# A three-stage decoder kernel: selected rows by indexed DMA, a new order of the steps, scores on four row strips, and one table for exp and ln

## The chip, the cores and the metric

The kernel runs on one core of a Trainium2 chip. The metric is the device time of one execution in microseconds; the median of the runs is given. The core has five engines, each with its own instruction queue: TensorE (PE in the profile, PEld its weight loads), VectorE (DVE), ScalarE (ACT), GpSimd (POOL) and SyncE (SP), which only issues DMAs here.

## The reference

Sixteen independent sequences (batch rows) of 256 tokens by 256 features pass through three stages, all in float32.

```python
x = x + attn(layernorm(x), w_attn, w_proj)          # stage a: causal linear attention, 16 heads of 16
x = x + xattn(layernorm(x), ctx, ctx, W_diff, ...)  # stage b: divergence attention over tanh probabilities, exact-gelu MLP 256-1024-256
x = x + ffn(layernorm(x), w_router, W_qkv, ...)     # stage c: below

def ffn(x, ...):                                    # CAP = 128 of the 256 tokens of a row
    scores = x @ w_router
    _, idx = top_k(scores, CAP)                     # ranks the tokens, ties by the smaller index
    x_sel = take_along_axis(x, idx)
    h = rmsnorm(x_sel, g1); q, k, v = h @ W_qkv.T   # 16 heads of 16, causal softmax attention over the 128
    x_attn = softmax(mask(q @ k.T / 4)) @ v @ W_out.T
    h2 = rmsnorm(x_sel + x_attn, g2)
    x_ff = silu(h2 @ W1.T) * (h2 @ W2.T) @ W3.T     # 682 wide
    return x.at[idx].set(x_sel + x_attn + x_ff)     # the other tokens keep x
```

## The kernel before

A batch row has its 256 tokens as two blocks (TT) of 128 partitions. The work is cut into some 170 named steps, `a_...`, `b_...` and `c_...` by stage. One text, `ORDER`, lists all of them; every engine runs through this list and executes the steps that it has a function for, so the list fixes the order in each engine's queue, while the times follow from semaphores. The list is one round. In round i stage a works on row i, stage b on row i-1, stage c on row i-2, and each `+` behind a name moves the step one row further back. The rounds that fill and drain the pipeline are written out; the others are a loop (`rounds`). An engine executes its queue strictly in order, so a step that waits holds back all behind it.

Large products with weights (`a_q`, `a_k`, `a_val`, `a_proj`, `b_up_*`, `b_down_*`, `c_gu_*`, `c_ff_*`) are split in a high and a low part and made of three passes. The others are plain float32; each such matmul stands in the trace as two records. PSUM has eight banks: a0, a1, a2 for stage a, b0, b1 for b, c0, c1, c2 for c.

Stage c, to which most of the change belongs, does the top-k and the gather by matrices. `c_rscore` (L938) makes the router scores as a column, `c_sbc` (L1298) spreads them over the partitions, `c_before` (L950) compares all pairs with a mask for ties, and `c_rank` (L1308, L1311) adds up the comparisons on TensorE to the rank of each token, as a row and as a column. `c_sel` and `c_selu` (L958, L965, L967) build three selection matrices, one scaled by the rms. `c_ht` (L1319) multiplies the normalised rows by the scaled one, which gives the selected rows transposed. `c_qk`, `c_v` and `c_score_0/1` (L1351 the mask, L1356 the products, 32 rows of the array each) follow; a score step fills two banks for 8 of the 16 heads, `c_max` takes row maxima, `c_exp` (L652) makes exponentials with their sum, one instruction a head, and `c_etp`, `c_etput` transpose them for `c_att`. `c_xo` (L1393, L1398) puts the selected rows (by the unscaled matrix) and the output projection in one bank. After the gated feed-forward, `c_scat` (L1469) multiplies the result, in two parts, by the third matrix, and `c_done` (L1032) adds it to `c_ob` (L975), the rows that were not selected. SyncE stores the result of the row. `x2`, the input of stage c, is started by GpSimd in `b_kept` (L402).

Stage a's scores `a_score_0/1` (L1166) use four row strips and four banks at a time. `keep_clock` (L1475) issues matmuls whose result nobody reads, 14 at the start and others at the places in `WARM_AT`, all in the first and the last rounds.

ScalarE needs a table load (ACT_TABLE_LOAD) where it goes to a function that the table in force does not hold. In a round of the kernel before, these stand at `a_qout` (exp, L532), `b_log` (ln, L589), `b_sexp` (exp, L602) and `b_gelu_0` (gelu, L615); the tanh of `b_tanhk`, `b_tanhq` (L571) and `c_tanh` (L691) has none.

## Time and profile before

| | |
|---|---|
| median of 3 runs | 951.96 us (951.67 to 952.5) |
| span of the profiled execution | 947.8 us |
| busy: PE, PEld, DVE, ACT, POOL | 883.4, 750.3, 727.6, 595.2, 218.6 us |
| mean granted TensorE clock | 0.995 of full speed |
| DMA | 25.05 MB, 26 GB/s over the span |

The span is that of the profiled execution, from its first to its last instruction; the median is of other executions and includes what lies around the span, 4.2 us here. Busy time is the union of an engine's instructions; the time that one instruction takes is longer than its distance to the next where they overlap. "Idle before" is time in which the engine waited, and the name behind the arrow is what released it.

### The profile page before, as it was taken

How to read it: one execution, taken by the hardware profiler on the slowest of the kernel's cores; microseconds unless marked ns; L12 is line 12 of the kernel's file. 1: busy time of each engine (PE TensorE's matmuls, PEld its weight loads, DVE VectorE, ACT ScalarE, POOL GpSimd, SP SyncE). 2: the span in 40 equal slices, each digit the busy share in tenths (PEclk: the TensorE clock that was granted, in tenths of full speed). 3: DMA queues.
4: the chain of work that ended last, by engine and by line, in shares of the span. 5: the costliest groups of instructions: out<-in, count | busy, mean ns of one | idle time of the engine just before them, and what ended most of it. 6: DMA issues, size and time to landing. Idle time of an engine off the chain costs nothing.

```text
span 947.8 us, 21833 instructions
## 1 busy us (share of the span) xinstructions
PE 883.4 (93%) x7652; PEld 750.3 (79%) x7652; DVE 727.6 (77%) x1670; ACT 595.2 (63%) x1582; POOL 218.6 (23%) x379
## 2 busy tenths in 40 slices
PE   7888999999999999999999999999999999998987
PEld 4657797978879797887979788787979788786855
DVE  4878878787887878888787879788787878866342
ACT  4365757667574767657575766757576675745533
POOL 0215122121313122221312222231321222121100
PEclk9999999999999999999999999999999999999999
DMA  7220100101010100101010010101000010000000
GB/s 261 68 82 2 35 1 13 35 12 33 11 33 0 37 7 11 33 11 33 0 44 0 11 33 11 33 11 33 0 17 28 11 33 22 12 2 11 2 13 12
DMA packets 20465, 25.05 MB, mean 26 GB/s; under 512 B 1488, under 2 KB 18000, under 8 KB 20432
## 3 DMA queue, kind: packets, MB, share of 16 engines
q1 hardware_dynamic: 18992, 20.33, 6.6%
q10 hardware_dynamic: 1440, 4.28, 1.4%
q8 instruction: 20, 0.33, 0.1%
q14 instruction: 13, 0.11, 0.0%
HBM read 20.41 MB, written 4.19 MB: 26 GB/s over the span
## 4 chain that ended last, share of the span: by engine, by line
PE 64%; DVE 20%; ACT 7%; issue 7%; DMA 1%; POOL 0%; DVEq 0%; SPq 0%; ACTq 0%; POOLq 0%
PE bank L1064 21%; PE bank L1370 4%; PE bank L1166 4%; PE bank L1356 4%; PE bank L1331 3%; PE bank L1245 3%; PE bank L1253 3%; PE bank L1424 2%; DVE before L950 2%; ACT L615 2%; PE bank L1319 2%; PE bank L1184 2%; PE bank L1457 2%; PE bank L1080 2%; DVE prob L850 2%
## 5 line engine op out<-in xcount | busy, mean ns | idle before, releaser
L652 ACT ACTIVATE w_raw_or_stage_c<-bank,c_nmax 128x128 f32<-128x128 f32 x256 | 90.6, 375 | 12.3 <-DVE c_nmax L981 12.3
L615 ACT ACTIVATE prob<-bank,b_folded 128x256 f32<-128x256 f32 x128 | 53.7, 471 | 46.0 <-PE bank L1064 45.8
L981 DVE TENSOR_REDUCE c_nmax<-bank 128x4 f32<-128x512 f32 x64 | 43.5, 683 | 48.1 <-PE bank L1356 48.1
L809 DVE TENSOR_TENSOR a_s<-bank,const 128x512 f32<-128x512 f32 x112 | 71.8, 677 | 9.0 <-PE bank L1166 6.4
L729 DVE TENSOR_TENSOR b_s_lo<-prob,b_s_hi 128x512 fp32r<-128x512 f32 x64 | 54.2, 848 | 27.3 <-ACT b_s_hi L503 27.3
L426 POOL TENSOR_TENSOR a_tr_lo<-a_norm,a_tr_hi 128x512 fp32r<-128x512 f32 x16 | 21.0, 1310 | 216.9 <-ACT a_tr_hi L503 216.9
L402 POOL TENSOR_TENSOR x<-x,vectors_by_row 128x512 f32<-128x512 f32 x16 | 20.7, 1292 | 161.7 <-DVE w_raw_or_stage_c L975 161.7
L652 ACT ACTIVATION_READ_ACCUMULATOR w_raw_or_stage_c<-bank,c_nmax 128x1 f32 x256 | 55.1, 215 | 0.0
L799 DVE RECIPROCAL a_e<-a_e 128x512 f32<-128x512 f32 x16 | 53.4, 3340 | 0.0
L1064 PE MATMUL bank<-b_s_hi,w_mlp_hi 128*128 128x256 f32 x256 | 44.8, 298 | 4.8 <-ACT prob L615 4.6
L1475 PE MATMUL bank<-ones_bf 128*128 128x512 bf16 x164 | 46.7, 410 | 1.0 <-POOL ones_bf L400 1.0
L691 ACT ACTIVATE w_raw_or_stage_c<-bank,c_rms_half 128x384 f32<-128x384 f32 (+1 forms) x32 | 17.2, 537 | 47.7 <-PE bank L1072 43.7
L503 ACT ACTIVATE b_s_hi<-prob 128x512 fp32r<-128x512 f32 x64 | 40.4, 632 | 9.9 <-PE bank L1064 9.3
L503 ACT ACTIVATE w_raw_or_stage_c<-bank 128x512 f32<-128x512 f32 x32 | 19.1, 598 | 43.7 <-PE bank L1370 43.7
L1370 PE MATMUL bank<-const,w_raw_or_stage_c 128*128 128x128 f32 x256 | 41.0, 283 | 2.0 <-ACT c_et L503 0.7
L1064 PEld LDWEIGHTS bank<-b_s_hi,w_mlp_hi 128*128 128x128 f32 x256 | 34.5, 189 | 10.2 <-ACT prob L615 8.8
L402 POOL TENSOR_TENSOR q_bias<-b_f,vectors_by_row 128x512 f32<-128x512 f32 x16 | 20.9, 1305 | 86.6 <-DVE b_f L875 86.6
L1370 PEld LDWEIGHTS bank<-const,w_raw_or_stage_c 128*128 128x128 f32 x256 | 27.5, 141 | 16.8 <-issue 12.3
L1064 PE MATMUL bank<-w_mlp_hi,b_s_lo 128*128 128x256 f32 x256 | 40.2, 279 | 0.0
L1064 PE MATMUL bank<-b_s_lo,w_mlp_hi 128*128 128x256 f32 x256 | 40.1, 279 | 0.0
L1064 PE MATMUL bank<-w_mlp_hi,b_s_hi 128*128 128x256 f32 x256 | 40.1, 278 | 0.0
L1064 PE MATMUL bank<-w_mlp_lo,b_s_hi 128*128 128x256 f32 x256 | 40.1, 278 | 0.0
(257 smaller groups left out, 2818.4 us busy)
## 6 DMA issues: line engine op xcount, KB each, us to landing
x_in<-in_x SPq DMA_DIRECT2D x16, 256.0 KB, 2.7
qc<-in_ctx SPq DMA_DIRECT2D x16, 256.0 KB, 3.2
b_f<-in_ctx_t SPq DMA_DIRECT2D x16, 256.0 KB, 3.4
out<-w_raw_or_stage_c SPq DMA_DIRECT2D x16, 256.0 KB, 2.1
w_raw_or_stage_c<-in_w ACTq DMA_DIRECT2D x4, 512.0 KB, 5.4
w_raw_or_stage_c<-in_w_gu ACTq DMA_DIRECT2D x4, 341.0 KB, 3.0
w_raw_or_stage_c<-in_w_a SPq DMA_DIRECT2D x2, 384.0 KB, 4.5
w_raw_or_stage_c<-in_w ACTq DMA_DIRECT2D x2, 384.0 KB, 4.4
```

What stands on the lines that cost most here:

```text
L402: add_bc = lambda out_, in_, vec: nc.gpsimd.tensor_tensor(out_, in_, vec.unsqueeze(1).broadcast_to([P, TT, D]), ALU.add)
L503: act_in(out_, in_, ACT.Copy, scale=scale).then_inc(done.sem, 1)
L615: act_in(prob[:, 2 * (j % 2) + n, :], b0[:, n * T:(n + 1) * T], ACT.Gelu, bias=b1p[:, f:f + 1]).then_inc(b_gelu.sem, 1)
L652: act_in(c_e[g % 2][:, j * R:(j + 1) * R], (c1, c2)[g % 2][:, j * R:(j + 1) * R], ACT.Exp, bias=c_nmax[:, n:n + 1], accum_out=c_den[:, hea ...
L729: tt(out_, full, high.bitcast(F32), ALU.subtract).then_inc(done.sem, 1)
L799: nc.vector.reciprocal(a_e1[:, :], a_e1[:, :]).then_inc(a_dinv.sem, 1)
L809: tt(heads(A_MASKED[t][n][:, :]), heads(A_SCORES[n][:, :]), tri.unsqueeze(1).broadcast_to([P, 4, P]), ALU.mult).then_inc(a_scput.sem, 1)
L981: nc.vector.tensor_reduce(c_nmax[:, 4 * g:4 * g + 4], heads((c1, c2)[g % 2][:, :]), axis=AX.X, op=ALU.max, negate=True).then_inc(c_max.sem, 1)
L1064: last = mm(out_, lhs(o, p, k), rhs(o, q, k), start=begin and a == 0 and o == 0 and k == 0, stop=end and a == len(passes) - 1 and k == n - ...
L1166: last = mm(A_SCORES[n][:, 2 * c * P:2 * (c + 1) * P], kT[r:r + 32, c, t * P:(t + 1) * P], qM[r:r + 32, c, t, :, :].rearrange("p m q -> p ...
L1370: last = nc.tensor.transpose(c0[:, j * R:(j + 1) * R], c_e[g % 2][:, j * R:(j + 1) * R], ident)
L1475: mm(heads((c2 if i < B else a0)[:, :]), ones_bf[:, :], ones_bf[:, :].unsqueeze(1).broadcast_to([P, 4, P]), start=True, stop=True)
```

## The change

The ranks are now made on VectorE alone: `c_rank` compares and adds up in one instruction for each token block. `c_sel` makes one selection matrix in bf16, and `c_idx` multiplies it by the token numbers, which gives the token number of each slot. SyncE stores normalised rows, residual rows and the rms, side by side, to a buffer in DRAM (`store_rows`, 256 rows of 513 numbers); GpSimd fetches the 128 selected ones by an indirect DMA (`c_pick`). `c_hsc` scales them and `c_ht` transposes them. The base of the output, `c_ob`, is now made on GpSimd for all tokens and stored as soon as it is there, and the 128 results are written over it by a second indirect DMA (`c_put`). `c_hx` on GpSimd adds the residual that goes with them; `c_h2put` moves from ScalarE to VectorE. The scores are made in one step on four row strips into the banks c0, c1, c2 and a2; this makes `a_k` and the score step wait for steps of other rows. `a_qout` asks for the table that holds exp and ln. `WARM_AT` is empty. `ORDER` is new, and its greatest shift is one more, so there is one more round. SyncE's queue has a new order too.

```diff
 ORDER = """
-a_y+ c_w2 c_att+ b_up_1+ b_down_0+ b_up_2+ c_dput+ b_gelu_1+ a_yhi+ b_ghi_1+ a_mean c_o+ b_glo_1+ c_w3 c_w0
-b_gelu_2+ a_done+ c_xo+ c_h2put+ c_h2lo+ b_mean b_ghi_2+ c_h2hi+ b_gelu_3+ a_proj+ b_glo_2+ a_normed b_ghi_3+
-c_w4 c_h2tp+ b_glo_3+ c_gate_0+ b_normed b_kept+ b_o+ b_omean+ c_gate_1+ b_fb2+ a_kept+ b_frstd+ b_up_3+
-b_down_1+ c_gu_0+ a_ylo+ c_h2rms+ c_gtlo_0+ a_rstd b_onormed+ b_down_2+ b_down_3+ c_gu_1+ b_tanhk b_rstd
-c_tanh_0+ b_qb c_tanh_1+ c_gu_2+ c_gthi_0+ c_gtp_0+ c_gtp_1+ c_ff_0+ a_tp b_done+ c_gthi_1+ a_thi c_gtlo_1+
-c_mean a_tlo c_y+ b_tanhq c_ff_1+ b_v b_pnorm c_ylo+ c_yhi+ b_vput c_normed a_q c_scat+ a_k a_qout c_sbc
-c_done+ b_orstd+ c_rscore a_kout b_diff c_before a_val c_rank b_log b_dtp a_ktp a_phi_q a_phi_k c_sel a_vput
-c_hput b_vq c_ht b_rtp b_ratio c_qk c_selu a_csum b_sid c_score_0 b_dput a_kput a_kq c_ob c_max_0 b_rput
-a_mask a_sput c_qkput b_sexp a_state c_exp_0 c_max_1 b_fput c_w5 a_dput b_fmean a_scput_0 a_scput_1 a_den b_fd
-c_v c_exp_1 c_vput c_w6 c_etput_0 a_scput_2 a_score_0 c_etp_0 c_score_1 a_scput_3 c_w7 c_w1 c_etp_1 c_max_2
-c_etput_1 a_score_1 b_htp b_fnormed a_att_0 c_etp_2 c_exp_2 c_w8 a_scput_4 b_hhi c_max_3 b_hlo c_rstd c_rms1
-a_scput_5 a_scput_6 c_dinv b_up_0 a_scput_7 c_exp_3 c_etput_2 c_etp_3 a_dinv c_dtp c_dbc c_etput_3 b_glo_0
-b_gelu_0 b_ghi_0 c_w9 a_att_1
+c_w2 a_kput+ c_ff_0++ c_ff_1++ c_gtlo_1++ c_rstd+ c_ht+ a_score_0+ b_fput+ b_fmean+ b_htp+ a_sput+ c_hsc+
+b_sexp+ c_gthi_0++ b_fnormed+ c_gthi_1++ a_mask+ a_mean a_dput+ c_w7 a_scput_0+ b_hlo+ a_scput_1+ c_qk+
+c_hput+ c_w1 b_up_0+ a_scput_2+ a_scput_3+ a_score_1+ c_w3 c_y++ c_rms1+ c_v+ a_scput_4+ b_hhi+ a_att_0+ c_w4
+c_qkput+ b_gelu_0+ a_scput_5+ a_scput_6+ b_up_1+ a_scput_7+ a_att_1+ b_ghi_0+ b_gelu_1+ b_glo_0+ a_dinv+
+c_vput+ a_y+ b_glo_1+ b_ghi_1+ b_down_0+ b_up_2+ b_gelu_2+ c_score+ b_up_3+ c_w8 a_proj+ a_yhi+ b_ghi_2+ c_w9
+c_h2rms++ c_max_0+ c_max_1+ b_down_1+ b_down_2+ b_gelu_3+ b_qb+ c_etp_0+ c_max_2+ c_exp_0+ c_hx++ b_down_3+
+b_glo_2+ a_done+ c_max_3+ b_ghi_3+ c_exp_1+ c_etp_1+ c_ob+ b_v b_mean c_exp_2+ a_tp b_glo_3+ a_normed b_normed
+b_kept+ c_etp_2+ c_etput_0+ c_w0 c_exp_3+ c_w5 b_o+ c_etp_3+ c_dtp+ c_att+ b_omean+ b_onormed+ c_dinv+ b_done+
+c_etput_1+ c_xo+ c_dbc+ c_mean c_keep+ c_pick+ c_o+ c_etput_2+ a_tlo c_etput_3+ c_normed c_h2put+ c_dput+ a_q
+a_thi b_tanhk b_tanhq c_h2tp+ a_kept+ c_h2sq+ a_k c_rscore b_pnorm c_sbc c_gu_0+ c_h2lo+ b_vput b_fb2+ c_h2hi+
+a_val c_idx a_qout b_diff b_frstd+ b_dtp c_put++ c_gu_1+ b_rtp a_rstd a_ylo+ c_rank b_log c_gu_2+ c_gtp_0+
+c_sel a_ktp b_vq b_sid c_gtp_1+ a_state b_rstd b_fd c_idxput b_orstd+ c_tanh_0+ a_kout b_ratio c_gate_0+
+a_phi_q a_phi_k b_dput c_gate_1+ b_rput c_w6 a_csum a_kq c_gtlo_0+ c_tanh_1+ a_den a_vput
 """.split()
 SKEW = {"a": 0, "b": 1, "c": 2}
 STEPS = [(name.rstrip("+"), SKEW[name[0]] + name.count("+")) for name in ORDER]
...
+WARM_AT = {}
 WARM_START = 14
...
+        sel = sb("select_by_token", [P, TT, R], BF16)
+        index = sb("row_of_slot", [P, 1], mybir.dt.uint32)
+        index_out = sb("row_of_slot_out", [P, 1], mybir.dt.uint32)
+        batch_at = sb("first_row", [P, 1])
...
+        C_SCORES, EXP_T = (c0, c1, c2, a2), (c0, c1, c0, c2)
+        EXP_T_FREE = (4, 8, 12, 16)
...
+            def store_rows(b):
+                sp.wait_ge(*c_normed(b))
+                sp.sem_inc(passed.sem, 1)
+                sp.wait_ge(*c_rms1(b))
+                sp.sem_inc(passed.sem, 1)
+                if not first(b):
+                    sp.wait_ge(*picked_in(b - 1))
+                    sp.sem_inc(passed.sem, 1)
+                sp.dma_start(token_rows_by_p, rows[:, :, 0:W]).then_inc(rows_out.sem, 16)
...
+            with sp.Fori(2, B - 1) as i:
+                next_ctx(i - 1)
+                store_rows(i - 2)
+                store(i - 2)
+                next_ctx_t(i - 1)
                 next_x(i)
-                next_ctx(i - 1)
-                next_ctx_t(i - 1)
-                store(i - 2)
...
+            def c_ob_(b):
+                pool.wait_ge(*c_normed(b))
+                if not first(b):
+                    pool.wait_ge(*out_done(b - 1))
+                nc.gpsimd.tensor_tensor(ob[:, :, :], x2, c_norm, ALU.add).then_inc(c_ob.sem, 1)
+
+            def c_pick_(b):
+                pool.wait_ge(*c_idxput(b))
+                pool.wait_ge(*rows_out(b))
+                if not first(b):
+                    pool.wait_ge(*c_hx_s(b - 1))
+                    pool.wait_ge(*c_h2put(b - 1))
+                pool.sem_inc(passed.sem, 1)
+                nc.gpsimd.indirect_dma_start(
+                    picked[:, 0:W], None, token_rows[:, :], bass.IndirectOffsetOnAxis(ap=index[:, 0:1], axis=0)) \
+                    .then_inc(picked_in.sem, 16)
+
+            def c_hx_(b):
+                pool.wait_ge(*c_h2put(b))
+                pool.wait_ge(*picked_in(b))
+                if not first(b):
+                    pool.wait_ge(*c_y(b - 1))
+                nc.gpsimd.tensor_tensor(c_hx, c_h2[:, :], x2_sel, ALU.add).then_inc(c_hx_s.sem, 1)
+
+            def c_put_(b):
+                pool.wait_ge(*c_y(b))
+                pool.wait_ge(*c_kept(b))
+                pool.wait_ge(*out_done(b))
+                pool.sem_inc(passed.sem, 1)
+                nc.gpsimd.indirect_dma_start(
+                    out[:, :], bass.IndirectOffsetOnAxis(ap=index_out[:, 0:1], axis=0), y_out, None) \
+                    .then_inc(y_stored.sem, 16)
 
...
             def a_qout_(b):
+                nc.scalar.preload_act_table_set("natural_log_exp_and_others")
                 act_e.wait_ge(*a_qk(b, 1))
...
+            def c_h2sq_(b):
+                act_e.wait_ge(*c_h2put(b))
+                act_in(flat(c_hT[:, :, :]), c_h2[:, :], ACT.Square, scale=1.0 / D ** 0.5, accum_out=c_sq2[:, :]) \
+                    .then_inc(c_h2sq.sem, 1)
...
-            def c_before_(b):
+            def c_rank_(b):
                 dve.wait_ge(*c_sbc(b))
...
+                for t in range(TT):
+                    if t:
+                        dve.wait_ge(*c_rank(b, t))
+                    stt(tie[:, :], b0[:, 0:T], c_sc[:, t:t + 1], tie_bound[:, t, :], ALU.subtract, ALU.is_gt,
+                        accum_out=c_rk[:, t:t + 1]).then_inc(c_rank.sem, 1)
...
             def c_sel_(b):
...
+                if not first(b):
+                    dve.wait_ge(*c_idx(b - 1))
                 for t in range(TT):
+                    dve.wait_ge(*c_rank(b, t + 1))
+                    ts(sel[:, t, :], iota_bf[:, :], c_rk[:, t:t + 1], None, ALU.is_equal).then_inc(c_sel.sem, 1)
...
+            def c_idxput_(b):
+                dve.wait_ge(*c_idx(b))
+                if not first(b):
+                    dve.wait_ge(*picked_in(b - 1))
+                nc.vector.tensor_copy(index[:, :], b0[:, T:T + 1]).then_inc(c_idxput.sem, 1)
+
+            def c_hsc_(b):
+                dve.wait_ge(*picked_in(b))
+                ts(c_h[:, :], x_sel, r1_sel, None, ALU.mult).then_inc(c_hsc.sem, 1)
+
+            def c_keep_(b):
+                if not first(b):
+                    dve.wait_ge(*y_stored(b - 1))
+                    dve.wait_ge(*c_next(b - 1))
+                ts(index_out[:, :], index[:, :], batch_at[:, 0:1], None, ALU.add).then_inc(c_kept.sem, 1)
+                dve.wait_ge(*c_kept(b))
+                ts(batch_at[:, :], batch_at[:, :], float(T), None, ALU.add).then_inc(c_next.sem, 1)
 
             def c_max_(g):
...
+            def c_h2put_(b):
+                dve.wait_ge(*c_xo(b))
+                tt(c_h2[:, :], c2[:, 0:D], x_sel, ALU.add).then_inc(c_h2put.sem, 1)
...
+            def c_idx_(b):
+                pe.wait_ge(*c_sel(b))
+                for t in range(TT):
+                    last = mm(b0[:, T:T + 1], sel[:, t, :], token_bf[:, t:t + 1], start=t == 0, stop=t == TT - 1)
+                last.then_inc(c_idx.sem, 1)
+
...
-            def c_ht_(b):
-                pe.wait_ge(*c_sels(b))
                 for c in range(DC):
-                    for t in range(TT):
-                        last = mm(c0[:, c * R:(c + 1) * R], c_norm[:, t, c * P:(c + 1) * P], sel_s[:, t, :],
-                                  start=t == 0, stop=t == TT - 1)
+                    last = nc.tensor.transpose(c0[:, c * R:(c + 1) * R], c_h[:, c * P:(c + 1) * P], ident)
                 last.then_inc(c_ht.sem, 1)
...
+            def c_score_(b):
+                pe.wait_ge(*c_qkput(b))
+                pe.wait_ge(*c_vput(b))
+                if not first(b):
+                    pe.wait_ge(*c_y(b - 1))
+                if not at_least(b, B - 2):
+                    pe.wait_ge(*a_scput(b + 2, 7))
+                for bk in C_SCORES:
+                    mm(heads(bk[:, :]), ident_bf[:, :], mask_bf[:, :].unsqueeze(1).broadcast_to([P, 4, P]),
+                       start=True, stop=False, skip_group_check=True)
+                for c in range(DC):
+                    for n, bk in enumerate(C_SCORES):
+                        r = 32 * n
+                        last = mm(bk[:, 2 * c * R:2 * (c + 1) * R], cq[r:r + 32, c, :],
+                                  ck[r:r + 32, c, :, :].rearrange("p m k -> p (m k)"), start=False, stop=True,
+                                  skip_group_check=True)
+                last.then_inc(c_score.sem, 1)
```

The comparison, the selection and the scatter of before (`c_before`, the old `c_rank`, `c_selu`, `c_yhi`, `c_ylo`, `c_scat`, `c_done`) are removed; `b_dtp` also waits for `c_idxput` of the row before, since both use bank b0, and `b_kept` and `c_normed` wait for the store of the row before.

## Rows read from the trace of the kernel before

**Rows 1.** Windows of busy time: a steady round, the second round, the drain.
```profile
49.42:94.57 45.15, 39.38 (x322) 30.87 (x323) 36.97 (x80) 26.66 (x50) 15.65 (x24) 1.00 0.15 44
...
422.06:476.45 54.39, 51.87 (x467) 45.45 (x468) 44.41 (x104) 36.46 (x98) 13.24 (x23) 1.00 0.06 19
...
857.64:947.80 90.16, 76.81 (x538) 56.21 (x536) 37.22 (x94) 40.61 (x126) 9.56 (x20) 1.00 0.02 8
```
The columns are: window, its length, then busy time and instructions of PE, PEld, DVE, ACT and POOL, the granted clock, the DMA share and GB/s. Each window ends where a row's logarithm (`b_log`) starts.

**Rows 2.** Chain of waits, one steady round: start, length, what it ran over.
```profile
423.90 1.16 PE bank L1319 x8
...
429.74 1.06 PE bank L1356 x8
...
438.73 1.12 PE bank L1166 x16
...
444.83 1.28 ACT L615
...
446.12 0.85 ACT prob L615 x2
...
447.02 4.42 PE bank L1064 x36
451.44 0.86 PE bank L1393 x4
...
454.54 0.22 PE bank L1405 x2
...
475.03 1.30 DVE before L950 x4
```

**Rows 3.** Timeline of TensorE, 417 to 423 us: start, length, instructions.
```profile
417.12 0.39 PE L1469 MATMUL bank<-c_hs_hi,select_by_rank 128*128 128x256 f32 x2
417.71 0.50 PE L1469 MATMUL bank<-c_hs_lo,select_by_rank 128*128 128x256 f32 x2 [0.19 <-DVE c_hs_lo L729]
...
421.99 0.51 PE L1308 MATMUL bank<-before,ones_bf 128*128 128x256 bf16 x4 [0.37 <-DVE before L950]
422.33 0.29 PE L1311 MATMUL bank<-ones_bf,before 128*128 128x1 bf16 x6
```

**Rows 4.** Timeline of ScalarE, the first 43 us.
```profile
0.73 1.28 ACT L701 ACT_TABLE_LOAD   x1 [0.73 <-PEq L1545]
...
13.86 0.60 ACT L532 ACTIVATE a_e<-bank 128x512 f32<-128x512 f32 x1 [1.95 <-PE bank L1064]
...
42.44 0.42 ACT L571 ACTIVATE prob<-qc 128x256 f32<-128x256 f32 x1 [2.77 <-DVE w_mlp_lo L725]
```

**Rows 5.** Groups of instructions on VectorE: busy us, mean ns, idle before.
```profile
L975 DVE SCALAR_TENSOR_TENSOR w_raw_or_stage_c<-w_raw_or_stage_c,c_unselected,x 128x256 f32<-128x256 f32 x32 | 14.0, 478 | 0.1
...
L938 DVE CUSTOM_DVE_ANT_0 c_rden_or_products<-w_raw_or_stage_c,vectors_by_row 128x256 f32<-128x256 f32 x32 | 13.5, 422 | 0.6
...
L1032 DVE TENSOR_TENSOR w_raw_or_stage_c<-w_raw_or_stage_c,bank 128x512 f32<-128x512 f32 x16 | 11.0, 687 | 0.8 <-PE bank L1469 0.8
```

**Rows 6.** DMA issues: count, KB each, median us to landing.
```profile
x_in<-in_x SPq DMA_DIRECT2D x16, 256.0 KB, 2.7
...
out<-w_raw_or_stage_c SPq DMA_DIRECT2D x16, 256.0 KB, 2.1
...
w_diff<-in_w_diff SPq DMA_DIRECT2D x1, 256.0 KB, 10.5
```

**Rows 7.** Groups of instructions on GpSimd.
```profile
L402 POOL TENSOR_TENSOR x<-x,vectors_by_row 128x512 f32<-128x512 f32 x16 | 20.7, 1292 | 161.7 <-DVE w_raw_or_stage_c L975 161.7
```

**Rows 8.** Groups of instructions, the whole run: the fillers.
```profile
L1475 PE MATMUL bank<-ones_bf 128*128 128x512 bf16 x164 | 46.7, 410 | 1.0 <-POOL ones_bf L400 1.0
```

**Rows 9.** A window of the drain; columns as in rows 1.
```profile
850.00:860.00 10.00, 8.98 (x51) 6.25 (x50) 8.40 (x29) 3.35 (x4) 2.28 (x6) 0.87 0.08 26
```

**Rows 10.** Chain of waits in the drain, the last row alone.
```profile
918.32 3.45 PE bank L1475 x16
...
924.82 2.90 ACT w_raw_or_stage_c L652 x16
```

242 lines of the change are left out of this document (84 added, 158 removed).

## The prediction, written before the changed kernel was run

> **What bounds the kernel now.** I began with the windows of busy time, cut from one row's logarithm on ScalarE to the next: these are whole rounds. A steady round lasts 54.39 us; in it TensorE is busy 51.87 us, VectorE 44.41, ScalarE 36.46, GpSimd 13.24 [rows 1]. From 94.57 to 857.64 us there are 14 rounds of 54.5 us; before them lie 94.6 us in which the pipeline fills, behind them 90.2 us in which it drains [rows 1]. So in a steady round TensorE sets the time and idles only 2.5 us. The chain of waits agrees: it runs mostly over TensorE's products and leaves them in a few places, one of which is VectorE's ranking (L950, 1.30 us), another the load of the gelu table (L615, 1.28 us) [rows 2]. A step taken off TensorE is therefore worth its own length; one taken off another engine is worth something only where TensorE waits for it.
>
> **What leaves TensorE.** I count by the distance between starts, since matmuls overlap. Per batch row: the ranking's sums of comparisons (L1308, L1311) 0.50 us from 421.99 on; the gather of selected rows by a product (L1319) 1.16; the gather of the residual rows (L1393) 0.86; the scatter (L1469, two pairs) from 417.12 to 418.21, less its wait of 0.19 and an overlap with the next product of about 0.17, 0.74 [rows 2, 3]. Sum 3.26 us. The third stage's scores: today two steps of 8 records, 1.06 us each (L1356), on two row strips at a time. The first stage does 16 records on four strips in 1.15 us (L1166) [rows 2]. Four strips and four banks should do the same here: 2.12 - 1.15 = 0.97 us off. The four mask products stay.
>
> **What comes to TensorE.** The selected rows, now fetched, must be transposed: two transposes, 0.22 us as L1405's [rows 2]. The index of each slot is two products of one column, a third of L1311's six: 0.1 us at most [rows 3]. Net: 3.26 + 0.97 - 0.32 = 3.9 us less, 48.0 us busy.
>
> **VectorE.** Off: four comparisons 1.30 us, selectors about 1.5, the output's base 0.87 (two of L975 by their spacing), the last addition 0.69, a subtraction 0.41 (half-size row of the same kind) [rows 2, 5]: with small ones 4.7 us. On: two comparisons with a running sum, nearest L938 at 0.42 each plus its readout, so 1.1; two bf16 selectors at 0.1 to 0.28, so 0.3; the scaling 0.4; the residual sum 0.41; four tiny ones 0.5 [rows 5]. Sum 2.7, net 2.0 less: 42.4 us. ScalarE loses two 256-wide copies (0.8): 35.7 us. Neither is the longest, but VectorE at 42.4 of about 49.5 is as tight as before (44.4 of 54.4).
>
> **GpSimd and the DMAs.** It gains the output's base (1.29, as the same shape in L402), a half-size addition (0.7), and two indirect DMAs [rows 7]. No row here shows one. Below, nothing of theirs is seen if they hide; a 256 KB transfer takes 2.1 us (store) to 2.7 us (x) from issue to landing; above, the longest landing of this program is 10.5 us, behind other transfers [rows 6]. The gather moves 128 rows of 2 KB, again 256 KB. I take 4.5 us, near the x row with room for GpSimd's own work, and 2.1 and 10.5 as ends. Cover, walked through the new order by durations of rows: the index is ready about 21 us behind the end of b_up_3, where GpSimd has just done b_kept; the scaling c_hsc that needs the rows stands behind b_fput and b_fmean in VectorE's order, at about 31 us. Ten microseconds of cover against 4.5, so I cost it at nothing in a steady round; uncovered it is its full 4.5. The store of 256 rows into DRAM lies ahead of it and ends by 17 us. SP's queue now has, in this order, the context, this store, the output's store, the transposed context and x; x is issued last, after b_fd, at about 29 us, and lands at 32 us, just when a_mean wants it. That cover is thin: 0.3 us or so could be lost there.
>
> **Tables.** Four loads a round before (L532, L589, L602, L615). At the program's start, a load at 0.73 us serves an exponential at 13.86 and a tanh at 42.44, with no load between [rows 4]: so one table holds exp and tanh, and c_tanh, a_kout, c_tanh, b_sexp of the new order need one load together. After: one before gelu, one before c_exp, the explicit one, one before c_tanh: four again. What changes is where they lie. The logarithm follows a_qout without a load, and b_sexp without one, on which TensorE waited; in exchange c_exp_0 gets one, behind b_gelu_3. There ScalarE needs 0.84 + 1.28 + 1.45 = 3.6 us (four exponentials, half of 2.90 [rows 10]), while TensorE has a_proj, b_down_1 and b_down_2, three times 1.47 us (a third of 4.42) [rows 2]. The load hides with 0.8 us to spare.
>
> The rows price a load at its 1.28 us: it starts at 444.83 and the gelu behind it at 446.12 [rows 2]. The Trainium skill's page "ScalarE: Activation LUTs" (section "What ACT_TABLE_LOAD costs") says about 2.66 us for every switch, with the drain. By that page the load before c_exp_0 would miss its cover by 0.6 us a round, 8 us in all. I go by the row.
>
> **Idle time of the new order.** The old order idles 2.5 us. Walking the new one with durations from rows, TensorE waits for c_etput_3 before c_att (0.5 us), for c_o before c_xo (0.5), for c_idxput before b_dtp (0.4), for a_phi before a_ktp (0.3), at b_sexp and a_mask (0.3); 2.0 us together. Bounds: 0.6 if semaphores and queues smooth it, 3.5 if VectorE's order holds it up at a_score_1 and c_idx too. I take 1.8: a round of 48.0 + 1.8 = 49.8; bounds 48.6 and 51.5.
>
> **Fill and drain.** Today 184.8 us. The fillers cost 46.7 us of TensorE in all, mostly where it waits anyway; one group sits in the last chain, 3.45 us [rows 8, 10]. The last row's chain loses the matmul ranking and both gathers (3.3 us), one round trip of scores (2) and those fillers (3); it gains the trip to DRAM and back (2.1 + 4.5), and a scatter that ends 1.5 us later than a store. Those nearly cancel: -0.2. The clock: with fillers it was granted at 1.2 GHz for a part of 850 to 860 us (0.87 in that window), and at 2.4 behind it [rows 1, 9]. Without them TensorE idles longer in both ends, and some of its work there (about 105 us net of fillers) will run at 1.2. If a tenth of it does, that is 10 us more of work, of which I let half be hidden by the other engines' share of the chain: 5; bounds 0 and 25. In the first rounds the shorter third stage gives back 3. Head and tail: 184.8 - 0.2 + 5 - 3 = 187.
>
> **The sum.** 14 x 49.8 + 187 = 884 us of span. Before, the span was 947.8 and the median of the runs 951.96, 4.2 more; so 888 us. My walk through the order without its allowance gives 49.1 a round and 878; I take 882, between them, 7.3% faster. One measurement of this kernel can tell about 0.2% from no change.
>
> **Rivals.**
> 1. *VectorE's order becomes the bound.* It is busy 42.4 us, and its in-order queue serves three stages. For it: the wait chain leaves TensorE mostly to VectorE. Against: its busy share of a round rises only from 82 to 85%. Round 51.5 to 52.5, 14 x 2.2 = 31 us more: 913.
> 2. *The clock falls at both ends.* If a third of the work there runs at 1.2 GHz and nothing hides it, +25 us over my 5: about 905.
> 3. *The gather blocks (the slower one).* c_hsc stands in VectorE's queue ahead of b_fnormed, a_mean and all a_scput; of the gather's time G, what goes beyond the ten us of cover is lost each round. The forecast lies 70 us below before, 5.0 a round, so from G = 15 us on the kernel is slower; at 17 us it is 14 x 7 = 98 us over 882: 980. For it: no row shows an indirect DMA, and 10.5 us plus three operations of 1.29 us come to 14.4 [rows 6, 7]. Against: 256 KB land in 2.7 us.
> 5. *The change does nothing to the round*, because the removed steps only uncover waits: idle 6.4 us instead of 1.8. Removed work was on the chain, so this needs new waits of that size: 952.
>
> **Chances.** Forecast (863 to 900): 0.60. Rival 1: 0.13. Rival 2: 0.10. Rival 3: 0.06. Rival 4: 0.03. Rival 5: 0.03, split. The remaining 0.05 is a round shorter than 48.6 (below 863). Range: low end from rounds of 48.4 and a head and tail of 178, 856 + 4 = 860; the high end takes in rivals 1 and 2, 918. Outside lie the gather, rival 5 and some of the low case. Faster 0.91, same 0.01, slower 0.08.
>
> **What would show it.** Windows of one round: 49 to 50.5 us with TensorE at 48 busy. Sixteen score records in 1.15 us. c_hsc with no idle time before it on VectorE (else rival 3, with its length there). Four table loads a round. b_sexp and b_log without a load. Granted clock in the head and the tail: how many windows stand below 1. The forecast is wrong if c_score's records still pair, if x arrives after b_fnormed, or if VectorE is busy above 45 us a round.

## The result, and the profile after

The changed kernel takes 928.2 us (median of 4 runs, 924.3 to 929.9), the kernel before 952.2 beside it: ratio 0.9744, 95% interval 0.9717 to 0.977, so 2.6% faster. I had forecast 882 and a range of 860 to 918. The sign is right; the size is not: of 70 us forecast, 24 came. The profiled run took 929.9 us with a span of 928.1.

First the windows of the changed kernel, with the columns of [rows 1]. I cut them where the table load in front of `a_qout` starts, for rows 3 and 15, so that 12 rounds lie between; the same cuts of the kernel before lie at 144.32 and 797.44 us.

```profile
0.00:155.95 155.95, 120.21 (x928) 99.42 (x929) 110.89 (x231) 76.75 (x177) 37.44 (x61) 0.84 0.23 77
155.95:776.09 620.14, 577.67 (x5331) 513.16 (x5330) 530.75 (x1189) 423.39 (x1152) 223.98 (x325) 1.00 0.12 38
776.09:928.10 152.01, 118.89 (x897) 99.47 (x895) 83.63 (x191) 76.64 (x222) 39.69 (x59) 0.88 0.08 27
...
414.23:465.96 51.73, 48.24 (x447) 42.83 (x446) 44.27 (x100) 35.29 (x96) 18.67 (x28) 1.00 0.12 38
```

A round takes 620.14 / 12 = 51.68 us, and TensorE is busy 48.2 of it. That is the 48.0 of my sum. What I had not forecast is beside it: TensorE idles 3.5 us instead of 1.8, VectorE is busy 44.3 instead of 42.4 (as long as before, [rows 1], with four comparisons, two selectors and an output base fewer), and the granted clock is 0.84 and 0.88 at the ends. The kernel before, cut alike:

```profile
0.00:144.32 144.32, 127.70 (x1048) 100.75 (x1049) 111.30 (x233) 79.76 (x182) 36.82 (x60) 0.98 0.23 74
144.32:797.44 653.12, 622.71 (x5594) 545.70 (x5593) 533.06 (x1237) 437.65 (x1176) 159.07 (x277) 1.00 0.06 19
797.44:947.80 150.36, 132.96 (x1014) 103.81 (x1012) 83.23 (x202) 77.75 (x224) 22.69 (x43) 0.99 0.04 12
```

So the 12 rounds gained 33.0 us; the head gave 11.6 back and the tail 1.7. Next, all waits of TensorE of 0.2 us or more in one steady round of the changed kernel, in its timeline (the brackets hold the idle time and what ended it). The first three rows are taken one round later than the others:

```profile
471.03 0.20 PE L1359 MATMUL bank<-token_bf,select_by_token 128*128 128x1 bf16 x2 [0.42 <-DVE select_by_token L1014]
471.78 0.63 PE L1133 MATMUL bank<-const,b_f 128*128 128x128 f32 x4 [0.55 <-DVE row_of_slot L1020]
475.63 0.44 PE L1133 MATMUL bank<-const,kT 128*128 128x128 f32 x2 [0.80 <-DVE kT L830]
...
457.06 1.97 PE L1279 MATMUL bank<-w_diff,b_f 128*128 128x256 f32 x8 [0.47 <-DVE b_f L957]
461.07 0.30 PE L1421 MATMUL bank<-w_raw_or_stage_c,c_v_even 128*32 128x128 f32 x2 [0.52 <-ACT c_et L562]
462.79 1.10 PE L1438 MATMUL bank<-w_ffn_out,c_hT 128*128 128x256 f32 x4 [0.64 <-DVE c_hT L1048]
```

The sum is 3.4 us. The first three (`c_idx`, `b_dtp`, `a_ktp`, 1.77 us) wait for VectorE in one stretch. Here are VectorE and then GpSimd in that stretch, one round earlier:

```profile
415.71 1.45 DVE L920 TENSOR_TENSOR b_f<-prob 128x512 f32<-128x512 f32 x1
417.09 0.47 DVE L1006 SCALAR_TENSOR_TENSOR c_rden_or_products<-bank,c_sc,const 128x256 f32<-128x256 f32 x1
...
418.01 1.22 DVE L1014 TENSOR_SCALAR select_by_token<-iota_row_bf,c_rank_col 128x128 bf16<-128x128 bf16 x2
...
419.81 1.25 DVE L925 TENSOR_TENSOR b_f<-prob 128x512 f32<-128x512 f32 x1
...
422.10 1.14 DVE L830 SCALAR_TENSOR_TENSOR qT<-a_e,qT 128x512 f32<-128x512 f32 x1
423.16 0.68 DVE L830 SCALAR_TENSOR_TENSOR kT<-a_e,kT 128x512 f32<-128x512 f32 x1
```

```profile
415.14 1.47 POOL L427 TENSOR_TENSOR q_bias<-qc,vectors_by_row 128x512 f32<-128x512 f32 x1
416.57 1.20 POOL L530 TENSOR_TENSOR w_raw_or_stage_c<-c_h,picked_rows 128x256 f32<-128x256 f32 x1
417.73 1.29 POOL L512 TENSOR_TENSOR w_raw_or_stage_c<-norm_x_rms 128x512 f32<-128x512 f32 x1
419.24 1.28 POOL L427 TENSOR_TENSOR norm_x_rms<-x,vectors_by_row 128x512 f32<-128x512 f32 x1 [0.23 <-POOL w_raw_or_stage_c L512]
420.73 1.31 POOL L521 DMA_INDIRECT picked_rows<-token_rows,row_of_slot  x1 [0.22 <-POOL norm_x_rms L427]
422.06 0.62 POOL L447 COPY x<-x_in 128x512 f32<-128x512 f32 x1
```

The two phis have one shape: 1.14 us beside the x copy, 0.68 behind it. (A phi is the one operation of `a_phi_q` or `a_phi_k`.) Lay the ends of the two engines together. The x copy ends at 422.68, the first phi 0.56 later; `b_kept` (L427) ends at 420.52, L925 0.54 later; the bias addition ends at 416.61, L920 0.55 later; the output's base (L512) ends at 419.02, the two selectors 0.21 later. Each VectorE operation seems to begin only when GpSimd's ends. It is so in every row of the batch, not in this one alone: by the groups over the whole run the two subtractions (`b_diff`, `b_ratio`) average 1.35 and 1.17 us where the kernel before has 0.69 and 0.68, the first phi 1.06 against 0.68, while the second, which nothing lies beside, keeps its 0.68.

```profile
L920 DVE TENSOR_TENSOR b_f<-prob 128x512 f32<-128x512 f32 x16 | 21.7, 1354 | 0.1
...
L925 DVE TENSOR_TENSOR b_f<-prob 128x512 f32<-128x512 f32 x16 | 18.7, 1167 | 0.5 <-ACT prob L649 0.5
```

```profile
L862 DVE TENSOR_TENSOR b_f<-prob 128x512 f32<-128x512 f32 x16 | 11.1, 692 | 2.4 <-DVE c_sc L938 2.3
```

L1006, which reads PSUM and SBUF, takes its 0.47 us beside GpSimd. GpSimd's own operations get longer too: L530, which began while L920 ran, took 1.20 us here and 0.92 in experiments 4 to 7.

The Trainium skill says this on its page "SBUF — State Buffer" (section "SBUF: two separate sides"): VectorE and GpSimd share one pair of ports. A VectorE operation in a two-port mode needs it, and so does one with two SBUF inputs, this one only against a GpSimd operation that reads SBUF. Whichever engine starts first has the pair for its whole instruction, and the other is blocked. The trace agrees in the four pairs above: GpSimd's operation began 0.04 to 0.57 us before VectorE's each time. I had cited another part of that section for the gather and not applied this rule to the additions.

The new parts themselves went as forecast. Scores, gather, landing times and tables, from the timelines of TensorE and ScalarE, VectorE's `c_hsc` and the DMA issues of that round (KB, median us to landing):

```profile
x_in<-in_x SPq DMA_DIRECT2D x1, 256.0 KB, 3.0
...
picked_rows<-token_rows,row_of_slot POOLq DMA_INDIRECT x1, 3.7
```

```profile
L1401 PE MATMUL bank<-c_k_by_parity,c_q x16: 374/374/478, 447.3 to 448.1; 32*128 32x256 f32 x16
```

```profile
414.23 1.28 ACT L590 ACT_TABLE_LOAD   x1
418.28 1.28 ACT L746 ACT_TABLE_LOAD   x1
436.61 1.28 ACT L675 ACT_TABLE_LOAD   x1
450.95 1.28 ACT L712 ACT_TABLE_LOAD   x1
```

```profile
430.82 0.34 DVE L1024 TENSOR_SCALAR c_rden_or_products<-picked_rows 128x256 f32<-128x256 f32 x1
```

Sixteen score records run in one step (1.12 us in the chain of waits, at 895.07 us, where before there were two of 1.06, [rows 2]). The gather starts 10 us ahead of `c_hsc`, lands in 3.7 us, and `c_hsc` shows no idle time. There are four loads of 1.28 us, none at `b_log` or `b_sexp`.

Last, the ends. Two windows of the changed kernel with the granted clock in the third column from the end ([rows 9] shows the one low window of the old drain):

```profile
20.00:50.00 30.00, 21.27 (x145) 17.04 (x146) 22.42 (x34) 10.67 (x17) 2.49 (x4) 0.50 0.31 91
...
900.00:920.00 20.00, 15.77 (x96) 12.36 (x97) 4.91 (x12) 8.15 (x29) 1.92 (x5) 0.66 0.00 1
```

From 20 to 50 us TensorE ran wholly at 1.2 GHz; before, the same stretch had 0.94. At 0.84 over the head's 156 us and 0.88 over the tail's 152, it stood at 1.2 GHz for about 2 x 0.16 x 156 = 50 and 2 x 0.12 x 152 = 36 us.

### The profile page after: what moved, and what is told of

Its sections match the earlier page's. It is cut to its first block, busy times and chain, and to the rows that moved or that the text cites. A ratio compares the mean times of both kernels' runs of the same rounds, so it can differ in the third digit from the quotient of the medians.

```text
span 928.1 us, 20992 instructions
## 1 busy us (share of the span) xinstructions
PE 816.8 (88%) x7150; PEld 712.0 (77%) x7150; DVE 725.3 (78%) x1609; ACT 576.8 (62%) x1550; POOL 301.1 (32%) x443
## 4 chain that ended last, share of the span: by engine, by line
PE 35%; DVE 22%; issue 17%; POOL 11%; ACT 10%; DMA 3%; POOLq 1%; DVEq 0%; SPq 0%; ACTq 0%
PE bank L1117 10%; DVE a_s L867 4%; PE bank L1239 4%; ACT w_raw_or_stage_c L712 3%; PE bank L1221 3%; PE bank L1301 2%; ACT L712 2%; PE bank L1309 2%; PE bank L1401 2%; DMA x_in<-in_x 2%; PE bank L1279 2%; PE bank L1385 2%; PE bank L1396 2%; POOL f_rs L436 1%; DVE prob L908 1%
## 5 line engine op out<-in xcount | busy, mean ns | idle before, releaser
L867 DVE TENSOR_TENSOR a_s<-bank,const 128x512 f32<-128x512 f32 x112 | 72.6, 685 | 42.1 <-PE bank L1239 22.2
L712 ACT ACTIVATION_READ_ACCUMULATOR w_raw_or_stage_c<-bank,c_nmax 128x1 f32 x256 | 62.5, 244 | 0.0
L784 DVE TENSOR_TENSOR b_s_lo<-prob,b_s_hi 128x512 fp32r<-128x512 f32 x64 | 44.9, 702 | 17.2 <-ACT b_s_hi L562 17.2
L427 POOL TENSOR_TENSOR q_bias<-b_f,vectors_by_row 128x512 f32<-128x512 f32 x16 | 20.6, 1286 | 116.0 <-DVE b_f L933 116.0
L1037 DVE TENSOR_REDUCE c_nmax<-bank 128x4 f32<-128x512 f32 x64 | 41.0, 684 | 21.0 <-PE bank L1401 21.0
L537 POOL DMA_INDIRECT out<-w_raw_or_stage_c,row_of_slot_out x16 | 17.4, 1090 | 98.0 <-DVE w_raw_or_stage_c L1085 98.0
L1117 PEld LDWEIGHTS bank<-b_s_hi,w_mlp_hi 128*128 128x128 f32 x256 | 34.4, 188 | 13.6 <-issue 10.8
L1221 PE MATMUL bank<-qT_by_parity,kT 32*128 32x256 f32 x512 | 39.5, 425 | 5.1 <-DVE a_e L867 2.6
L1412 PE MATMUL bank<-const,w_raw_or_stage_c 128*128 128x128 f32 x256 | 37.3, 278 | 7.5 <-ACT w_raw_or_stage_c L712 4.9
L1117 PE MATMUL bank<-w_mlp_hi,b_s_hi 128*128 128x256 f32 x256 | 43.4, 291 | 0.0
L1117 PE MATMUL bank<-b_s_hi,w_mlp_lo 128*128 128x256 f32 x256 | 40.2, 280 | 0.0
L1279 PE MATMUL bank<-w_diff,b_f 128*128 128x256 f32 x128 | 33.0, 403 | 7.5 <-DVE b_f L957 7.5
L1412 PEld LDWEIGHTS bank<-const,w_raw_or_stage_c 128*128 128x128 f32 x256 | 29.6, 143 | 9.5 <-ACT w_raw_or_stage_c L712 9.4
```

What stands on the lines that cost most here:

```text
L712: act_in(c_e[g % 2][:, j * R:(j + 1) * R], C_SCORES[g][:, j * R:(j + 1) * R], ACT.Exp, bias=c_nmax[:, n:n + 1], accum_out=c_den[:, head:he ...
L784: tt(out_, full, high.bitcast(F32), ALU.subtract).then_inc(done.sem, 1)
L867: tt(heads(A_MASKED[t][n][:, :]), heads(A_SCORES[n][:, :]), tri.unsqueeze(1).broadcast_to([P, 4, P]), ALU.mult).then_inc(a_scput.sem, 1)
L1037: nc.vector.tensor_reduce(c_nmax[:, 4 * g:4 * g + 4], heads(C_SCORES[g][:, :]), axis=AX.X, op=ALU.max, negate=True).then_inc(c_max.sem, 1)
L1117: last = mm(out_, lhs(o, p, k), rhs(o, q, k), start=begin and a == 0 and o == 0 and k == 0, stop=end and a == len(passes) - 1 and k == n - ...
L1221: last = mm(A_SCORES[n][:, 2 * c * P:2 * (c + 1) * P], kT[r:r + 32, c, t * P:(t + 1) * P], qM[r:r + 32, c, t, :, :].rearrange("p m q -> p ...
```

## The experiments

Thirteen kernels ran. Three questions: what do the fillers carry, what lengthens VectorE's operations, and what are the other waits? "Round" is always the stretch between the `a_qout` loads of rows 3 and 15, over 12.

**1. The old kernel without its fillers.**

```
-WARM_AT = {(0, "a_q"): 2, (0, "a_ktp"): 1, ... (18, "c_scat"): 3}
+WARM_AT = {}
```

> The kernel before with its 164 single fillers left out (the 14 at the start stay), everything else as it was: one part of the change alone. Clock theory: without them TensorE is granted 1.2 GHz in stretches of the first 120 and the last 100 us, as in the changed kernel's trace (about 51 and 39 us of it), and the time rises by 10 to 25 us, to 962 to 977; the steady round stays at 54.4. Rival (my own sum priced the ends at +5, -3 of it saved): the fillers lay mostly in the way, the time stays within 947 to 957.

964.7 us, ratio to the kernel before 1.0144 (1.0122 to 1.0167). Its windows:

```profile
0.00:150.27 150.27, 121.77 (x983) 102.16 (x984) 111.50 (x233) 80.00 (x183) 36.81 (x60) 0.88 0.22 71
150.27:803.02 652.75, 622.38 (x5594) 545.05 (x5593) 533.17 (x1237) 438.18 (x1176) 159.18 (x277) 1.00 0.06 19
803.02:961.50 158.48, 124.70 (x929) 103.82 (x927) 83.08 (x202) 77.95 (x224) 23.22 (x43) 0.88 0.04 11
```

The rounds stand still; the head is 6.0 us longer, the tail 8.1, and both at 0.88. By the medians the fillers were worth 13.4 us to the old kernel, within what I had expected.

**2. The changed kernel with fillers.** They stand where its own trace shows TensorE waiting.

```
-WARM_AT = {}
+WARM_AT = {(0,"a_tp"):6, (0,"a_q"):5, (1,"a_score_0"):9, (1,"a_proj"):10, (2,"c_idx"):16, ...
+           (16,"c_dtp"):8, (16,"c_idx"):8, (17,"b_htp"):5, (18,"c_etp_0"):9, (18,"c_etp_2"):5, ...}
```

> The changed kernel with 74 fillers of the same shape put where its own trace shows TensorE waiting in the first rounds and 71 where it waits in rounds 16 to 18. Clock theory: the granted clock stays at 1.00 in nearly all stretches of 10 us at both ends, the head to the table load of row 3 falls from 156 to 146 to 149 us, the tail behind row 15's load from 152 to 145 to 149, the steady round stays at 51.7; the time falls from 928 to 911 to 920. Rival: the ends are set by VectorE and ScalarE chains, the clock rises and the time stays at 925 to 930.

917.4 us, ratio 0.9649 (0.9609 to 0.969) where the changed kernel had 0.9744.

```profile
0.00:150.30 150.30, 127.64 (x1029) 95.21 (x1030) 111.29 (x231) 76.65 (x177) 37.49 (x61) 0.98 0.25 80
150.30:770.18 619.88, 577.36 (x5331) 513.01 (x5330) 530.83 (x1189) 423.85 (x1152) 224.27 (x325) 1.00 0.12 38
770.18:914.40 144.22, 123.71 (x970) 96.83 (x968) 84.03 (x191) 76.69 (x222) 39.81 (x59) 0.99 0.09 29
```

The ends are 5.7 and 7.8 us shorter, the clock there 0.98 and 0.99, the rounds the same. With experiment 1 this confirms the clock theory both ways, though the head stayed above the 146 to 149 us that I had expected. One thing more can be read off: with fillers the head is 150.3 against the old one's 144.3, and the tail 144.2 against 150.4; without them the head is 155.95 against 150.3, the tail 152.0 against 158.5. Head and tail together are as long as the old ones (294.5 and 294.7 with fillers, 308.0 and 308.8 without). That the head alone is 6 us longer can be the place of the cut, since `a_qout` stands elsewhere in the new order; no run separates the two.

**3. GpSimd's four wide operations on 8 columns.**

```
-                add_bc(x2[:, :, :], x1[:, :, :], ln_b_bc).then_inc(b_kept.sem, 1)
+                few = slice(0, D if first(b) else 8)
+                nc.gpsimd.tensor_tensor(x2[:, :, few], x1[:, :, few], ...).then_inc(b_kept.sem, 1)
```

and likewise `b_qb`, `c_ob` and `c_hx`, from the second row on. This kernel leaves out most of their work, so its output is not the reference's; its waits and semaphores are those of the changed kernel.

> The changed kernel with four of GpSimd's wide operations (q_bias, x + bias, out rows, picked rows) made on 8 columns only from the second row on, so that work of 1.2 to 1.5 us each is left out of every round and the output is not the reference's; waits and semaphores stay. Contention theory: VectorE's operations with two SBUF inputs that ran beside them fall back (b_diff 1.45 to 0.69 us, b_ratio 1.25 to 0.69, the two selectors from 1.22 to about 0.3; phi_q 1.14, beside the x copy, may stay or fall), VectorE's busy time per round falls from 44.3 to 41.5 to 42.5, TensorE's waits before c_idx, b_dtp and a_ktp (0.40, 0.55, 0.81) shrink to under 0.8 together, the round from 51.7 to 50.0 to 50.8, the time to 900 to 915. Rival: these operations are slow by themselves (the data type, the new line), the times of the rows stay and so does the round.

907.9 us, ratio 0.9544 (0.9524 to 0.9564); round 50.42. VectorE in the same stretch:

```profile
406.79 0.68 DVE L924 TENSOR_TENSOR b_f<-prob 128x512 f32<-128x512 f32 x1
...
408.32 0.41 DVE L1018 TENSOR_SCALAR select_by_token<-iota_row_bf,c_rank_col 128x128 bf16<-128x128 bf16 x2
...
410.11 0.69 DVE L929 TENSOR_TENSOR b_f<-prob 128x512 f32<-128x512 f32 x1
...
411.83 0.69 DVE L834 SCALAR_TENSOR_TENSOR qT<-a_e,qT 128x512 f32<-128x512 f32 x1
412.45 1.09 DVE L834 SCALAR_TENSOR_TENSOR kT<-a_e,kT 128x512 f32<-128x512 f32 x1
```

Every slow row shown above fell back, and VectorE is busy 42.11 us in that round, which took 50.11 (42.2 on the mean of the twelve). The x copy, left at full size, now starts at 412.14 and hits the other phi; it takes 0.85 us itself instead of 0.62, since the first phi had begun before it. The slow operation is the one that overlaps, not one of a kind. Contention is shown. It is worth 1.26 us a round here, and TensorE still idles 2.4.

**4 to 7. The same with no work left out.** If only the overlap costs, moving GpSimd's operations must do what shrinking them did. It took four steps, and each miss showed in the trace where the cost went next. First: `b_qb` behind `b_rstd`, `b_frstd` ahead of `b_fb2`, and

```
-... b_qb+ ... c_hx++ ... c_ob+ ... b_kept+ ... c_pick+ ... a_kept+ b_fb2+ b_frstd+
+... c_hx++ c_pick+ c_ob+ b_kept+ a_kept+ b_frstd+ b_fb2+ ... b_rstd b_qb
             def c_ob_(b):
+                if not at_least(b, B - 2):
+                    pool.wait_ge(*a_phi(b + 2))
```

> The changed kernel with only GpSimd's order changed, nothing left out: q_bias directly behind b_rstd, the copy of the picked rows and the gather first, out rows, x + bias and the x copy only after VectorE's second phi, f_rs ahead of the next q_bias. Contention theory: the same gain as with the operations cut down, less what the gather's descriptors and the picked rows still cost: round 50.2 to 51.0, time 905 to 918. Rival (the order of TensorE's own chain binds): the rows get faster, the round stays above 51.3, time 922 to 930.

925.6 us, round 51.41: a miss; both lie in the range that I had given to TensorE's own chain. The two subtractions (0.90 and 0.69), the selectors (0.41) and both phis (0.68) are back, but the three operations of GpSimd that wait now lie beside the scan, which takes 2.31 us for two instead of 1.27:

```profile
417.83 2.31 DVE L850 TENSOR_TENSOR_SCAN a_e<-kT 128x256 f32<-128x256 f32 x2
```

Second, with the wait on `a_kq`, the product behind the scan:

> As the kernel in which GpSimd's order was changed, but out rows, x + bias and the x copy wait for VectorE's product behind the scan (a_kq) and not for its second phi: in that run they had moved onto the scan, which took 2.31 us for two instead of 1.27, and c_ht and b_htp waited 0.43 and 0.75. Contention theory: the scan falls back to 1.27, a_kq from 0.92 to 0.69, both new waits go, the round falls from 51.38 to 50.0 to 50.6, the time from 925.5 to 903 to 914. Rival: GpSimd's later end now delays something else (f_rs, the x load), the round stays above 51.

914.4 us, round 50.83, just outside the ranges that I had expected. The scan is at 1.27 again. But GpSimd's bias addition (start 425.13, 1.25 us) lies beside the normalisations, 1.68 us instead of 0.74, and TensorE waits for them:

```profile
425.19 1.68 DVE L801 TENSOR_SCALAR prob<-b_f,f_mv,f_rs 128x256 f32<-128x256 f32 x2 [0.93 <-POOL f_rs L436]
```

Third, `b_fb2` behind `a_rstd`:

> As the last kernel with GpSimd's order changed, and GpSimd's bias addition of the third stage's input (q_bias from b_f, 1.25 us) moved from behind f_rs to behind a_rs, where VectorE reads PSUM: in the last run it lay beside the two normalisations into prob, which took 1.68 us instead of 0.74, and b_htp waited 0.76 for them. Contention theory: they take 0.74 again, the wait before b_htp goes to 0.1 or less, VectorE's busy time is 42.1, and with all of GpSimd's work done the round equals that of the kernel in which it was cut down: 50.0 to 50.3 (from 50.80), time 903 to 910. Rival: only what was left out there gave that round; it stays at 50.6 or more.

912.9 us, round 50.82: a miss again, and an instructive one. VectorE is busy 42.11 us in the round from 410.09 us, as with the work cut down; no row of this stretch is slow any more. What took the gain is a transfer:

```profile
427.85 0.75 DVE L791 BATCH_NORM_STATS2 a_st<-x_in 128x6 f32<-128x256 f32 x2 [0.95 <-DMA x_in<-in_x]
```

The x copy ends later, SP issues the next x load only then, and in VectorE's queue `a_mean` stands in front of what the second stage needs; `b_up_0` waits 0.77. Fourth, `a_mean` from ahead of `a_scput_0` to behind `c_y`:

> As the kernel with the bias addition behind a_rs, and VectorE's a_mean moved from ahead of the score masks to behind c_y. In that run VectorE's slow rows were all gone (busy 42.11 a round, as in the kernel with the work cut down), but the round stayed at 50.74: the x copy ends 1.6 us later in the round, the x load with it, VectorE waited 0.95 for it before a_mean, and b_up_0 waited 0.77 for b_s_lo behind that. If the late x load is what took the rest of the gain: that wait and the 0.77 go, the round falls to 50.0 to 50.2, the time from 913 to 902 to 907. Rival: the wait moves to a_scput_0 and b_hlo anyway (they wait for TensorE), round 50.5 or more, time 909 or more.

895.8 us, ratio 0.9407 (0.9385 to 0.943); round 49.71, less than the 50.0 to 50.2 that I had expected: the step from 50.82 is 1.1 us, the wait that I had named 0.77, and TensorE is also busy 0.26 us less. All that TensorE waits for in a round:

```profile
406.27 0.63 PE L1135 MATMUL bank<-const,b_f 128*128 128x128 f32 x4 [0.34 <-DVE row_of_slot L1022]
442.02 1.96 PE L1281 MATMUL bank<-w_diff,b_f 128*128 128x256 f32 x8 [0.47 <-DVE b_f L959]
446.03 0.30 PE L1423 MATMUL bank<-w_raw_or_stage_c,c_v_even 128*32 128x128 f32 x2 [0.52 <-ACT c_et L564]
447.75 1.10 PE L1440 MATMUL bank<-w_ffn_out,c_hT 128*128 128x256 f32 x4 [0.64 <-DVE c_hT L1050]
```

That is 1.97 us. With GpSimd's steps mostly where VectorE reads PSUM, and `a_mean` further back, the order idles what my walk had given it. What `a_mean`'s new place alone would do to the changed kernel, no run shows; there neither `a_mean` nor `b_up_0` waits.

**8. The load ahead of `c_exp_0`.** I suspected it of making `b_v` wait, and swapped `c_exp_0+` and `b_ghi_3+`.

> The changed kernel with one pair swapped on ScalarE: b_ghi_3 ahead of c_exp_0 and its table load. If the table load makes b_o late, the wait of 0.47 before b_v goes and the round falls by up to 0.5 us, to 51.2, the time to 921 to 926. If b_v waits for the end of b_down_3 and the one VectorE addition of 0.68 behind it, the wait and the round stay (51.6 to 51.8), the time at 925 to 930.

971.8 us, ratio to the kernel before 1.0202 (1.017 to 1.0235); round 54.60. Both expectations were wrong. On ScalarE `b_ghi_3` has to wait 2.05 us for `b_down_1` to free its buffer. In the changed kernel the table load and the first exponentials run inside that wait; behind it, they come too late for the transposes:

```profile
473.47 0.66 PE L1412 MATMUL bank<-const,w_raw_or_stage_c 128*128 128x128 f32 x4 [2.19 <-ACT w_raw_or_stage_c L712]
```

So putting the exponentials inside the gelu phase is sound, and one pair swapped costs 2.9 us a round: 2.2 of idle time and 0.7 of TensorE being busy longer (48.9 us against 48.1). The granted clock over those 12 rounds was 0.99.

**9. A new order around `c_att`.** `a_tp` and `c_etp_2` ahead of `b_v`, `a_q` between `c_att` and `c_xo`, `a_k` and `a_val` ahead of `c_gu_0`, ScalarE's copies ahead of `c_dbc`, `b_dtp` behind `c_gu_1`.

> The changed kernel with another order around the third stage's product with v: on TensorE a_tp and c_etp_2 ahead of b_v, c_dtp and a_q between c_att and c_xo, a_k and a_val ahead of c_gu_0, b_dtp behind c_gu_1; ScalarE's copies for c_att ahead of c_dbc. Chain theory: the waits before b_v, c_att and c_xo (0.47, 0.52, 0.64 us, the same in every variant of GpSimd's order) are bare latencies with nothing to run in them; they shrink to 0.5 or less in sum, and the round falls by 0.8 to 1.6 us to 50.1 to 50.9, the time to 906 to 917. Contention as the bound (VectorE 44.3 busy, slowed where c_idx, b_dtp and a_ktp wait): what is gained there turns up as longer waits before c_idx, b_dtp and a_ktp, the round stays above 51.3, the time at 922 to 930.

945.9 us; round 52.73, a miss by both theories. The waits before `b_v` and `c_xo` went, but `c_idx` waited 1.75 us, `c_att` 0.69 for ScalarE. Of the 1.05 us that a round got longer, 0.3 are idle time of TensorE and 0.7 its longer busy time (48.9 us); the granted clock over the 12 rounds was 0.98.

**10 to 13. Together.** The fillers with experiment 5's order and experiment 9's:

> All three edits together: fillers at both ends, GpSimd's wide operations behind a_kq, and the new order around c_att. If the three causes are separate, their gains add: ends 13 us less, round 51.7 less 1.3 (contention) less 1.2 (latencies), to 48.8 to 49.6, where TensorE's own 48 us are nearly all of it; time 880 to 893. If contention and latencies hide behind each other (either one alone leaves the other's wait in its place), the round is 49.8 to 50.6 and the time 893 to 905.

916.1 us, round 51.53, above both of my ranges: on experiment 5 the order of experiment 9 costs 0.7 us a round, on the changed kernel 1.05. Then two swaps alone on experiment 6 (`a_tp` ahead of `b_v`, `b_dtp` behind `c_gu_1`), with fillers:

> That kernel with the fillers at both ends and two swaps on TensorE: a_tp ahead of b_v, b_dtp behind c_gu_1. Fillers: 11 to 14 us less, as in their own run. Swaps: the waits before b_v (0.47) and b_dtp (0.34) go, c_att and c_xo still wait 0.52 and 0.64 (for ScalarE's last copies and VectorE's product): round 49.3 to 49.6. Time 883 to 892. If a_tp only uncovers the exponentials behind it (c_etp_3 waits for c_exp_3), the wait moves to c_etp_3 or c_att and the round stays at 50.0.

902.1 us, round 50.54 against 50.82, where I had expected 50.0 at most; and the same with `a_q` and `a_k` moved:

> The same with a_q between c_att and c_xo (a_thi ahead of c_dput on ScalarE, a_tlo ahead of c_o on VectorE) and a_k ahead of c_h2tp. If the wait before c_xo (0.64) is a bare latency, it goes, and nothing comes in its place: round 48.7 to 49.1, time 875 to 885. If it only moves (c_gu_0 or c_idx start later and VectorE's row of work behind them with it, as in the kernel with the larger change of order, where c_idx waited 1.75), the round is that of the kernel beside it or longer.

908.0 us, round 51.09: the wait before `c_xo` is gone and the round is longer. TensorE idles less (2.1 us a round against 2.4) but is busy 49.0 us instead of 48.1, at a clock of 1.00 in both; why stays open. Last, the second of these three kernels (902.1 us) with `a_mean` as in experiment 7 and `c_keep` behind `c_o`:

> The best kernel so far (902.1: fillers, GpSimd's order, two swaps on TensorE) with a_mean behind c_y and c_keep behind c_o. It waited 0.59 before b_up_0 (for b_s_lo, behind a_mean) and 0.89 before c_xo (c_o stood behind c_keep's two small operations, 0.36). If both are what they look like, the round falls from 50.61 to 49.6 to 49.9 and the time to 887 to 893. If the order has no such slack, each wait is replaced by one of the same size further on and the time stays at 898 to 905.

887.9 us, ratio to the kernel before 0.9353 (0.9327 to 0.938), the fastest of all, 4% under the changed kernel, and as expected in round and time.

```profile
0.00:147.43 147.43, 126.08 (x1029) 96.03 (x1030) 108.03 (x230) 76.83 (x177) 38.38 (x62) 0.98 0.25 81
147.43:744.00 596.57, 575.77 (x5331) 512.15 (x5330) 505.79 (x1189) 418.14 (x1152) 215.74 (x325) 1.00 0.13 40
744.00:885.80 141.80, 123.67 (x970) 97.01 (x968) 79.47 (x192) 76.32 (x222) 37.96 (x58) 0.99 0.09 29
```

Its round is 49.71, the same as in experiment 7. The swaps on TensorE gained nothing there: in the round from 395.82 us on, the waits before `b_dtp` and `b_v` are gone, but `a_ktp` waits 0.43 and TensorE is busy 48.03 us instead of 47.63. What this kernel has over experiment 7 comes from the ends, 5.3 and 5.5 us in the profiled runs (7.9 by the medians).

## Why the prediction was wrong

**The sum taken apart.** The forecast span was 14 x 49.8 + 187 = 884; it became 928.1 = 14 x 51.68 + 204.6. So the rounds cost 14 x 1.88 = 26.3 us more and head and tail 17.6 (204.6 is the span less 14 rounds). Another 6 us are my choice of 882 over the sum's own 888; that step went the wrong way, and the 49.1 us a round behind it have no derivation: the waits that my walk names add up to a round of 50.0. The 4.2 us between span and median went the other way. Wherever the runs give both, an execution takes 1.8 us more than its own span (929.9 and 928.1 here), so about 2.4 of the 4.2 only say that the profiled execution of the kernel before was faster than the median. In the changed kernel the median is 0.1 above the profiled span.

**What leaves and comes to TensorE: right.** 48.2 us against 48.0. **Scores on four strips: right** (1.12 against 1.15; the row of L1166 that I took it from says 1.12 too, [rows 2]). **Tables: right** in number and place; the load ahead of `c_exp_0` is hidden, and experiment 8 shows by what. It took 1.28 us and the next activation began 0.01 behind it, so of the prediction's two prices for a load the row's was right. **Gather: right.** 3.7 us against 4.5, 10 us of cover. Rival 3 did not come true: the two indirect DMAs hold GpSimd 1.31 and 1.10 us each and nothing waits for them in a steady round. The stall in the Trainium skill's box ("SBUF — State Buffer", section "SBUF: two separate sides") does not show in these rows.

**VectorE, the step that failed.** I put 42.4 us: removed and added operations, each at the duration of a row. Experiments 3 and 6 measured 42.2 and 42.1, so the count was good to 0.3 us. The changed kernel has 44.27, because here an operation's duration depends on what lies beside it. "GpSimd and the DMAs" had a sentence on what GpSimd gains (1.29 + 0.7 us and two indirect DMAs) and gave its additions no price. That is the term put at nothing without a reason. The additions, and those that GpSimd had before, now lie beside VectorE's two-input operations, in the one stretch where TensorE waits for VectorE. With four of them cut down the round is 1.26 us shorter (experiment 3), which is 17.6 of the 26.3 us; with all of them moved, and `a_mean` with them, 1.97 (experiment 7).

**The idle time, 1.8 against 3.5.** My walk named `c_att` 0.5 (0.52), `c_xo` 0.5 (0.64), `b_dtp` 0.4 (0.55), `a_ktp` 0.3 (0.80); it missed `c_idx` (0.42) and `b_v` (0.47), and nothing was lost at `b_sexp` and `a_mask`. With four of GpSimd's operations cut down the order as it stands idles 2.4 (experiment 3), and with them moved and `a_mean` further back 2.1 (experiment 7), so allowance and walk were near for a kernel without contention. The upper bound of 3.5 was exact, but I gave it to "VectorE's order", rival 1, at 0.13 and had no likely cause for it. Rival 1's place was right (`c_idx` and `a_ktp` wait for VectorE), its mechanism wrong: VectorE's order is not too full at 42.1.

**x's thin cover** I put at 0.3 us. In the changed kernel it holds: SP issued x at 429.79, it took 3.0 us, `a_mean` ran at 432.94 without a wait. It cost 0.95 in experiment 6, when the copy was moved.

**The clock: the term was mis-sized.** I set 5 us for it. By the ends' windows the fillers give back 13.4 us in the changed kernel (experiment 2; 10.8 by the medians, 9 by the ratios) and 14.1 in the old one (experiment 1; 13.4 by the medians), so 8.4 us of the 17.6 are this term. It is within my bound of 25. Rival 2 took a third of the work at 1.2 GHz; by time it was about 86 of 308 us.

**The rest of head and tail: a gain that did not come.** Without the clock I had 184.8 - 0.2 - 3 = 181.6. The kernel with fillers has 150.3 + 144.2 - 2 x 51.7 = 191.1, so 9.5 more. The old kernel, cut alike, has 144.3 + 150.4 - 2 x 54.4 = 185.8, one more than the 184.8 of my cuts; 3.2 are the gains that I had written and that did not come. The other 5.3 are two rounds' gain: of the sum's 14 rounds two lie in head and tail by these cuts, and the sum lets them shrink like the steady ones, while head and tail stayed as long as they were (294.5 us against 294.7). What holds them no experiment settled. The changed kernel's trace shows one wait of TensorE of 4.58 us for the first selectors at 110.20 us and one of 1.62 for the first gathered rows at 121.71.

Taken together, rivals 1 and 2 both came true in place, at 26 us over the rounds, of which experiment 3 ties 17.6 to contention, and at 13 us. I had priced each alone and had no case for both together.

## What to carry to other kernels

Before costing work moved to GpSimd at nothing, lay its operations beside VectorE's in time: where an operation of VectorE with two SBUF inputs began beside one of GpSimd's, it took its own duration and nearly all that was left of the other (0.12 to 0.15 us less than the sum here). That matters where TensorE waits for VectorE. Place GpSimd's work beside VectorE's PSUM reads, and after each move look at the next slow row, the DMA that the moved step releases, and what stands behind its consumer. Fillers that look like waste in the trace are priced by one run without them; here they were worth about 1.1 and 1.4% of the time.

## What the hardware showed unexpectedly

- VectorE on two SBUF inputs beside GpSimd: 0.68 became 1.45, 0.69 became 1.25, two scans 1.27 became 2.31, the two normalisations of one SBUF input 0.74 became 1.68, two bf16 selectors 0.41 became 1.22. The comparison that reads PSUM and SBUF kept its 0.47 beside GpSimd.
- An indirect DMA of 128 rows of 2 KB holds GpSimd 1.10 to 1.31 us and lands after 3.5 to 3.7; the scatter of 128 rows of 1 KB holds it 1.09 and lands after 2.5.
- The granted clock fell to 0.98 and 0.99 even in steady rounds where TensorE waited 1.75 or 2.19 us at one place.
